# Storing the last four field pairs of every second tile through DMAs of 123, 3 and 2 rows

## The chip, the cores and the metric

The kernel runs on one core of a Trainium2 chip. The metric is the device time of one launch in microseconds (us), the median of three runs. Profiled executions are single ones, and their own time is given beside them.

The core has five engines with their own instruction streams: PE (TensorE, matrix products), DVE (VectorE), ACT (ScalarE), POOL (GpSimd) and SP (SyncE, which here only issues DMAs). Data moves between HBM and the on-chip memory SBUF through 16 DMA engines. To keep them apart from the compute engines, the text calls them **lanes**. A DMA of 128 rows is cut into 8 rows for each of the 16 lanes, each lane works through its share in order, and the DMA has landed when the last of its lanes is done.

## The reference

```python
# x: (2048, 32, 64) f32, W: (496, 64, 64) f32, one matrix for each pair i < j of the 32 fields
xi = x[:, pi, :]
xj = x[:, pj, :]
proj = jnp.einsum('bpd,pod->bpo', xi, W)
return proj * xj
```

For each of the 496 pairs (i, j) the kernel projects field i with the pair's matrix and multiplies the result, element by element, with field j. The output has 2048 x 496 x 64 numbers in f32, 260 MB, against 25 MB of input.

## The kernel before

The batch is cut into 16 tiles of 128 rows. The matrices (`w_sb`) are loaded once and stay in SBUF. For each tile the 32 fields (`x_sb`, two buffers) are turned on PE with an identity (line 268), copied to `x_t` by ACT (line 234), and then go through 21 steps. A step fills two units of PSUM (`proj`, 128x1024 each): one for an even field, one for an odd one (line 290).

The products are made in two ways. DVE multiplies a unit straight from PSUM into the staging buffer (line 332). For about two thirds of the steps (`pool_steps`) the second unit is copied by ACT into the staging buffer (line 256) and multiplied there by POOL (line 219).

The steps form 11 groups with 61, 57, 53, 49, 45, 41, 37, 33, 54, 38 and 28 pairs. A group's pairs lie side by side in the output, so one DMA stores them: 128 rows, of 15,616 bytes each for group 0 and 7,168 bytes each for group 10. SP issues these stores in the order of the groups (line 189), one tile after the other, and waits before each for the engines that make the group (lines 184 to 188). The next tile's fields are loaded by a DMA that ACT issues (line 243).

There are nine staging buffers, called slots, for the eleven groups: groups 9 and 10 use the slots of groups 4 and 5 again (`SHARED_SLOTS`, line 17). Before a group is written into a slot, DVE and ACT wait until the slot's earlier stores have landed (`slot_free`, line 162). Each landed DMA adds 16 to the slot's semaphore `stored[k]`:

```python
eng.wait_ge(stored[k], tile.number * 16 * slot_uses[k] + 16 * len(before))
```

So in each tile group 9 waits for the landing of group 4's store of the same tile, and group 5 of the next tile waits for group 10's store. At the end SP waits for all the stores (line 207).

Of the kernel before, what the change touches and what calls it, by code (L numbers as in the profile page):

```python
# [9 lines left out]
P = 128  # L10
# [4 lines left out]
WARM_UP = 16  # L15

SHARED_SLOTS = {9: 4, 10: 5}


def pair_index(i, j, fields):  # L20
# [51 lines left out]
def field_pair_project(nc, x, w, ident, out, fields, dim):  # L72
    batch = x.shape[0]
    tiles = batch // P
# [11 lines left out]
    def items(tile):  # L86


        for n, item in enumerate(last_tile if tile.last else whole_tile):
            yield item, (1 + n) % 2, tile.number * per_tile + (1 + n) // 2  # L90
# [5 lines left out]
    def group_range(g):  # L96
        segments = [seg for s in groups[g] for unit in steps[s] for seg in unit]
        first = min(pair_index(i, j, fields) for i, j, _ in segments)
        assert sum(n for _, _, n in segments) == max(
            pair_index(i, j, fields) + n for i, j, n in segments) - first  # L100
        return first, sum(n for _, _, n in segments)

    slot_of = [SHARED_SLOTS.get(g, g) for g in range(len(groups))]
    slots = len(groups) - len(SHARED_SLOTS)
    assert sorted(set(slot_of)) == list(range(slots))
    slot_uses = [slot_of.count(k) for k in range(slots)]
# [12 lines left out]
    def every_tile(emit):  # L119

        for t in range(tiles):
            emit(Tile(t, t % 2, t // 2, last=t == tiles - 1))
# [9 lines left out]
    with ExitStack() as ctx:  # L132
        def sb(name, shape, dt=F32):
            return ctx.enter_context(nc.sbuf_tensor(name, shape, dt))

        def sem(name):
            return ctx.enter_context(nc.semaphore(name))
# [7 lines left out]
        staged = [sb(f"staged{k}", [P, slot_pairs[k] * dim]) for k in range(slots)]  # L145
# [12 lines left out]
        stored = [sem(f"stored{k}") for k in range(slots)]  # L158
# [3 lines left out]
        def slot_free(eng, tile, g):  # L162

            k = slot_of[g]
            before = [h for h in range(g) if slot_of[h] == k]
            if not (tile.first and not before):
                eng.wait_ge(stored[k], tile.number * 16 * slot_uses[k] + 16 * len(before))

        def staged_part(s, i, j, n):
            g = group_of[s]  # L170
# [3 lines left out]
        @block.sync  # L174
        def _(sp):
            def emit(tile):
                where = {item: (b, use) for item, b, use in items(tile)}
                for g, group in enumerate(groups):
                    first, n = group_range(g)


                    pooled = any(s in pool_steps for s in group)
                    if pooled and g == 0:
                        sp.wait_ge(pool_scaled[g], tile.number + 1)
                    b, use = where[group[-1]]
                    sp.wait_ge(emptied[b][group[-1] not in pool_steps], use + 1)
                    if pooled and g > 0:
                        sp.wait_ge(pool_scaled[g], tile.number + 1)  # L188
                    sp.dma_start(out[bass.ds(tile.number * P, P), first * dim:(first + n) * dim],
                                 staged[slot_of[g]][:, 0:n * dim]).then_inc(stored[slot_of[g]], 16)  # L190

            half = fields * dim // 2
            sp.dma_start(x_sb[0][:, 0:half], x[0:P, 0:half]).then_inc(x_first_loaded[0], 16)
            sp.dma_start(w_sb[:, w_cuts[0]:w_cuts[1]], w[:, w_cuts[0]:w_cuts[1]]).then_inc(w_loaded[0], 16)
            sp.dma_start(x_sb[0][:, half:], x[0:P, half:]).then_inc(x_first_loaded[1], 16)
            for c in range(1, len(w_cuts) - 2):
                sp.dma_start(w_sb[:, w_cuts[c]:w_cuts[c + 1]], w[:, w_cuts[c]:w_cuts[c + 1]]
                             ).then_inc(w_loaded[c], 16)

            c = len(w_cuts) - 2  # L200
            sp.dma_start(w_sb[0:dim, w_cuts[c]:w_cuts[c + 1]], w[0:dim, w_cuts[c]:w_cuts[c + 1]]
                         ).then_inc(w_loaded[c], 16)
            sp.dma_start(x_sb[1][:], x[P:2 * P, :]).then_inc(x_loaded[1], 16)

            every_tile(emit)
            for k in range(slots):
                sp.wait_ge(stored[k], 16 * slot_uses[k] * tiles)

        @block.gpsimd
        def _(pool):  # L210
# [17 lines left out]
        def _(act):  # L228
# [8 lines left out]
            def load_x(tile):  # L237

                _, b, use = list(items(Tile(tile.number - 1, 1 - tile.parity, None)))[-1]

                act.wait_ge(emptied[b][1], use + 1)
                act.wait_ge(pool_scaled[group_of[pool_steps[-1]]], tile.number)
                act.dma_start(x_sb[1 - tile.parity][:], x[bass.ds((tile.number + 1) * P, P), :]
                              ).then_inc(x_loaded[1 - tile.parity], 16)

            def emit(tile):
                for item, b, use in items(tile):
                    if item == LOAD_BEFORE and not tile.first and not tile.last:
                        load_x(tile)
                    if item == "turn":  # L250
                        turned_out(b, use, 1 - tile.parity)
                    elif item in pool_steps:
                        (i, j, n), = steps[item][1]
                        slot_free(act, tile, group_of[item])
                        act.wait_ge(filled[b][1], use + 1)  # L255
                        nc.scalar.activation(staged_part(item, i, j, n), proj[b][1][:, 0:n * dim],  # L256
                                             ACT.Copy).then_inc(emptied[b][1], 1)
# [58 lines left out]
        @block.vector  # L316
        def _(dve):
            def emit(tile):
                if tile.first:
                    for h in range(2):  # L320
                        dve.wait_ge(x_first_loaded[h], 16)
                for item, b, use in items(tile):
                    if item == "turn":
                        continue
                    slot_free(dve, tile, group_of[item])
                    for h in range(2):
                        if h and item in pool_steps:
                            continue
                        dve.wait_ge(filled[b][h], use + 1)  # L329
                        segments = steps[item][h]  # L330
                        for (i, j, n), at in zip(segments, place(segments, dim)):
                            last = nc.vector.tensor_tensor(  # L332
                                staged_part(item, i, j, n), proj[b][h][:, at:at + n * dim],
                                x_sb[tile.parity][:, j * dim:(j + n) * dim], ALU.mult)
                        last.then_inc(emptied[b][h], 1)

            every_tile(emit)
# [30 lines left out]
```

## Time and profile before

| | us |
|---|---|
| three runs | 690.97 to 691.70, median 691.17 |
| profiled execution | 690.77 |
| its span, first to last instruction | 689.0 |
| busy in it: PE / DVE / POOL / ACT | 597.5 / 414.4 / 390.8 / 205.2 |
| DMA packets' time, queue of SP and queue of ACT, as a share of 16 lanes' span | 93.5% and 5.7% |
| moved | 285.24 MB, mean 414 GB/s |

A busy figure of a compute engine says how long it was at work, not that the kernel had to wait for it. The share of the DMA lanes is a mean over the 16, so 6% of a stretch can mean one lane at work and fifteen idle. One row of one DMA is one packet in this kernel; the record of a packet overlaps the next one's on the same lane a little, so that the share of a fully busy stretch reads as 101% or 102%.

### The profile page before, as it was taken

To read this page: it belongs to the slowest core of one execution; us is meant where nothing else is said; L and a number is where in the kernel's file an instruction comes from. 1 tells how busy PE (TensorE), PEld (TensorE's weight loads), DVE (VectorE), ACT (ScalarE), POOL (GpSimd) and SP (SyncE) were. 2 spreads that over 40 slices of the span, in tenths; PEclk is the share of its full clock that TensorE was granted. 3 is DMA by queue.
4 is the path that set the end of the run, shared out by engine and by line. 5 is a ranking of instruction groups with operands and counts; after the bars stand their busy time and mean duration, and the time that the engine had idled before them with its cause. 6 is when DMAs were issued, how large, how long until landed. Compare 5 with 4: busy or idle time off the path is not lost.

```text
span 689.0 us, 7597 instructions
## 1 busy us (share of the span) xinstructions
PE 597.5 (87%) x2704; PEld 371.1 (54%) x2704; DVE 414.4 (60%) x528; ACT 205.2 (30%) x257; POOL 390.8 (57%) x228
## 2 busy tenths in 40 slices
PE   6969979799797989979799797989979799797972
PEld 4545655465464646646466564645646466464541
DVE  1647657485574756646576574856647576474851
ACT  2312414133241332414233241322414224141320
POOL 0745747566473755738557474755738557374751
PEclk9998989899897998989899898997989989898995
DMA  8999999999999999999999999999999999999897
GB/s 337 382 432 425 432 427 425 427 428 426 420 417 428 424 422 417 427 424 417 427 414 426 408 428 424 412 423 389 420 421 412 428 413 425 411 426 426 363 419 308
DMA packets 29765, 285.24 MB, mean 414 GB/s; under 512 B 3312, under 2 KB 3440, under 8 KB 7216
## 3 DMA queue, kind: packets, MB, share of 16 engines
q1 hardware_dynamic: 27584, 270.28, 93.5%
q10 hardware_dynamic: 2160, 14.75, 5.7%
q14 instruction: 16, 0.13, 0.0%
q8 instruction: 5, 0.08, 0.0%
HBM read 24.97 MB, written 260.05 MB: 414 GB/s over the span
## 4 chain that ended last, share of the span: by engine, by line
PE 48%; DMA 37%; POOL 5%; ACT 4%; DVE 3%; issue 1%; ACTq 0%; DVEq 0%; SPq 0%
PE proj L290 48%; DMA out_dram<-staged 36%; POOL staged L219 5%; ACT staged L256 4%; DVE staged L332 3%; DMA ident_sb<-ident_dram 1%; PE proj L307 1%; PE proj L268 0%; ACT x_t L234 0%; ACTq L255 0%; DVEq L132 0%; SPq L188 0%; DVEq L329 0%
## 5 line engine op out<-in xcount | busy, mean ns | idle before, releaser
L290 PE MATMUL proj<-w_sb,x_t 64*128 64x512 f32 (+7 forms) x2432 | 564.2, 564 | 71.8 <-DVE staged L332 69.5
L332 DVE TENSOR_TENSOR staged<-proj,x_sb 128x1024 f32<-128x1024 f32 (+7 forms) x528 | 414.4, 827 | 263.6 <-PE proj L290 186.4
L219 POOL TENSOR_TENSOR staged<-staged,x_sb 128x1024 f32<-128x1024 f32 (+4 forms) x224 | 390.6, 1755 | 283.1 <-ACT staged L256 281.4
L290 PEld LDWEIGHTS proj<-w_sb,x_t 64*128 64x128 f32 x2432 | 339.6, 205 | 289.3 <-issue 123.6
L256 ACT ACTIVATE staged<-proj 128x1024 f32<-128x1024 f32 (+4 forms) x224 | 172.9, 787 | 455.1 <-PE proj L290 348.1
L234 ACT ACTIVATE x_t<-proj 128x1024 f32<-128x1024 f32 x32 | 31.0, 1020 | 10.3 <-PE proj L268 9.8
L268 PEld LDWEIGHTS proj<-ident_sb,x_sb 128*128 128x128 f32 x256 | 28.2, 142 | 9.7 <-issue 7.6
L268 PE MATMUL proj<-ident_sb,x_sb 128*128 128x128 f32 x256 | 31.8, 278 | 1.5 <-DMA x_sb<-x_dram 1.5
L307 PE MATMUL proj<-ident_sb 128*128 128x128 f32 x16 | 3.7, 424 | 5.6 <-DMA ident_sb<-ident_dram 5.6
L307 PEld LDWEIGHTS proj<-ident_sb 128*128 128x128 f32 x16 | 3.3, 227 | 5.6 <-DMA ident_sb<-ident_dram 5.6
L234 ACT ACT_TABLE_LOAD x1 | 1.3, 1283 | 1.2 <-PEq L362 1.2
L362 POOL MEMSET const-float32-0.0<- 128x1 f32 x1 | 0.1, 98 | 0.2 <-issue 0.2
L362 POOL MEMSET const-bfloat16-1.0<- 128x1 bf16 x1 | 0.1, 101 | 0.0
L362 POOL MEMSET const-uint8-127<- 128x1 uint8 x1 | 0.1, 101 | 0.0
L362 POOL MEMSET const-float32-1.0<- 128x1 f32 x1 | 0.1, 98 | 0.0
## 6 DMA issues: line engine op xcount, KB each, us to landing
out_dram<-staged SPq DMA_DIRECT2D x16, 1952.0 KB, 11.4
out_dram<-staged SPq DMA_DIRECT2D x16, 1824.0 KB, 13.9
out_dram<-staged SPq DMA_DIRECT2D x16, 1728.0 KB, 17.0
out_dram<-staged SPq DMA_DIRECT2D x16, 1696.0 KB, 14.7
out_dram<-staged SPq DMA_DIRECT2D x16, 1568.0 KB, 14.1
out_dram<-staged SPq DMA_DIRECT2D x16, 1440.0 KB, 15.4
out_dram<-staged SPq DMA_DIRECT2D x16, 1312.0 KB, 15.5
out_dram<-staged SPq DMA_DIRECT2D x16, 1216.0 KB, 13.8
```

What stands on the lines that cost most here:

```text
L219: last = nc.gpsimd.tensor_tensor(product, product, x_sb[tile.parity][:, j * dim:(j + n) * dim], ALU.mult)
L234: nc.scalar.activation(x_t[to][:, h * (UNIT // P):(h + 1) * (UNIT // P), :].rearrange("p k b -> p (k b)"), proj[b][h][:], ACT.Copy).then_i ...
L256: nc.scalar.activation(staged_part(item, i, j, n), proj[b][1][:, 0:n * dim], ACT.Copy).then_inc(emptied[b][1], 1)
L268: last = nc.tensor.transpose(proj[b][h][:, n * P:(n + 1) * P], x_sb[of][:, k * P:(k + 1) * P], ident_sb[:])
L290: last = nc.tensor.matmul(proj[b][h][:, at:at + width], x_t[tile.parity][half, i // 2, :], w_sb[half, col:col + width], start=True, stop=True)
L307: nc.tensor.transpose(proj[1][0][:, 0:P], ident_sb[:], ident_sb[:])
L332: last = nc.vector.tensor_tensor(staged_part(item, i, j, n), proj[b][h][:, at:at + n * dim], x_sb[tile.parity][:, j * dim:(j + n) * dim], ...
L362: nc = bacc.Bacc("TRN2", target_bir_lowering=False, num_devices=1)
```

## The change

In tiles 1, 3, ..., 15 (`tile.parity`) group 10 is stored in four DMAs in the place of one. The first takes 24 of its 28 pairs for all 128 rows, now 6,144 bytes a row. The last four pairs, 1,024 bytes a row, follow in DMAs of 123, 3 and 2 rows. A DMA of 123 rows runs on 3 lanes with 41 rows each, one of 3 rows on 3 lanes, and one of 2 rows on 2 lanes, so the four pairs of an odd tile stay off the other lanes. Even tiles are stored as before. The semaphore counts are raised for the three DMAs more.

```diff
+SPLIT_GROUP = 10
+SPLIT_PAIRS = 4
+SPLIT_ROWS = (123, 3, 2)
...
         def slot_free(eng, tile, g):
...
-                eng.wait_ge(stored[k], tile.number * 16 * slot_uses[k] + 16 * len(before))
+
+                more = tile.half * len(SPLIT_ROWS) * (slot_of[SPLIT_GROUP] == k)
+                eng.wait_ge(stored[k], 16 * (tile.number * slot_uses[k] + more + len(before)))
...
-                    sp.dma_start(out[bass.ds(tile.number * P, P), first * dim:(first + n) * dim],
-                                 staged[slot_of[g]][:, 0:n * dim]).then_inc(stored[slot_of[g]], 16)
+                    whole = n - SPLIT_PAIRS if g == SPLIT_GROUP and tile.parity else n
+                    sp.dma_start(out[bass.ds(tile.number * P, P), first * dim:(first + whole) * dim],
+                                 staged[slot_of[g]][:, 0:whole * dim]).then_inc(stored[slot_of[g]], 16)
+                    if whole < n:
+                        row = 0
+                        for rows in SPLIT_ROWS:
+                            sp.dma_start(
+                                out[bass.ds(tile.number * P + row, rows), (first + whole) * dim:(first + n) * dim],
+                                staged[slot_of[g]][row:row + rows, whole * dim:n * dim]
+                            ).then_inc(stored[slot_of[g]], 16)
+                            row += rows
...
             for k in range(slots):
-                sp.wait_ge(stored[k], 16 * slot_uses[k] * tiles)
+                more = tiles // 2 * len(SPLIT_ROWS) * (slot_of[SPLIT_GROUP] == k)
+                sp.wait_ge(stored[k], 16 * (slot_uses[k] * tiles + more))
```

The change moves instructions on SP alone. At the seam from the last tile but one into the last, SP's stores stood like this (`staged5` is the slot of groups 5 and 10, `128x1792` are 128 rows of 1,792 numbers):

```order
L189 DMA out_dram<-staged4 128x2432
L189 DMA out_dram<-staged5 128x1792
```

Those are groups 9 and 10 of any tile. In the changed program the last tile ends so:

```order
L197 DMA out_dram<-staged4 128x2432
L197 DMA out_dram<-staged5 128x1536
L202 DMA out_dram<-staged5 123x256
L202 DMA out_dram<-staged5 3x256
L202 DMA out_dram<-staged5 2x256
```

Nothing changed places. One store became narrower, and three short ones stand behind it. In the odd tiles before the last, group 0's store of the next tile (`staged0`) comes after them.

## Rows read from the trace of the kernel before

**Rows 1.** The page: span, DMA by slices of the span, packets.

```profile
span 689.0 us, 7597 instructions
...
DMA  8999999999999999999999999999999999999897
GB/s 337 382 432 425 432 427 425 427 428 426 420 417 428 424 422 417 427 424 417 427 414 426 408 428 424 412 423 389 420 421 412 428 413 425 411 426 426 363 419 308
```

**Rows 2.** The page: the chain of work that ended last, by engine.

```profile
PE 48%; DMA 37%; POOL 5%; ACT 4%; DVE 3%; issue 1%; ACTq 0%; DVEq 0%; SPq 0%
```

**Rows 3.** That chain in order of time, one tile (start us, us, what).

```profile
533.19 15.18 DMA out_dram<-staged
548.38 0.02 issue
548.40 0.90 DVE staged L332
549.30 0.04 issue
549.35 14.98 PE proj L290 x50
...
564.41 1.03 ACT staged L256
...
565.48 5.79 PE proj L290 x22
...
572.37 2.10 POOL staged L219
...
574.52 15.21 DMA out_dram<-staged
```

**Rows 4.** Windows of one tile each: length, engines' busy time, PEclk, DMA share, GB/s.

```profile
75.70:117.00 41.30, 37.76 (x175) 23.46 (x173) 25.93 (x33) 13.64 (x18) 25.34 (x15) 0.92 1.01 428
...
282.60:324.00 41.40, 37.51 (x172) 23.14 (x170) 25.93 (x33) 12.99 (x17) 24.64 (x15) 0.92 1.00 421
...
530.70:572.00 41.30, 37.38 (x170) 23.14 (x169) 25.93 (x33) 12.72 (x17) 24.35 (x15) 0.92 1.00 420
572.00:613.40 41.40, 37.45 (x172) 23.27 (x171) 25.93 (x33) 12.99 (x17) 24.69 (x15) 0.92 1.01 421
```

**Rows 5.** The same view: a seam between tiles, and the last stores.

```profile
560.50:561.00 0.50, 0.50 (x6) 0.38 (x3) 0.50 (x1) 0.00 (x0) 0.50 (x1) 1.00 0.63 163
680.00:682.00 2.00, 0.00 (x0) 0.00 (x0) 0.00 (x0) 0.00 (x0) 0.00 (x0) 0.50 1.02 431
684.80:687.80 3.00, 0.00 (x0) 0.00 (x0) 0.00 (x0) 0.00 (x0) 0.00 (x0) 0.50 0.06 26
```

**Rows 6.** DMA view, the first 5 us: ACT's queue, rows of 512 bytes.

```profile
q10 hardware_dynamic: 143, 0.07, 5.1%
```

**Rows 7.** DMA view, 8 to 20 us: loads of the matrices.

```profile
DMA packets 1098, 5.04 MB, mean 420 GB/s; under 512 B 121, under 2 KB 121, under 8 KB 1098
...
q1 hardware_dynamic: 1098, 5.04, 102.1%
```

**Rows 8.** DMA view, 680 to 683 us: the last stores.

```profile
DMA packets 162, 1.28 MB, mean 428 GB/s; under 512 B 16, under 2 KB 16, under 8 KB 77
...
q1 hardware_dynamic: 162, 1.28, 102.2%
```

**Rows 9.** Waits from 530 to 571.3 us, one tile: total, times, longest.

```profile
DVE staged L332 <- DMA out_dram<-staged: 4.1, 1, 4.1
PE proj L290 <- DVE staged L332: 3.8, 1, 3.8
```

**Rows 10.** The issuing queue SP: its waits in the whole run.

```profile
SPq L188 <- POOL staged L219: 425.1, 144, 9.8
```

**Rows 11.** Line 189, the stores: what an issue takes (ns, min/median/max).

```profile
L189 SPq DMA_DIRECT2D out_dram<-staged x176: 332/332/384, 20.1 to 678.1; - x176
```

## The prediction
> **What bounds the kernel now.** I begin with the page's slices. The DMA lanes are at 9 tenths or more in nearly all of them, and the kernel moves 410 to 430 GB/s in most of them [rows 1]. The chain that ended last names PE for 48% and DMA for 37% [rows 2], which would make PE the larger part, so the chain has to be read in order of time. In one tile it runs: group 4's store, issued at 533.19, lands 15.18 us later; DVE can then reuse its slot, and 14.98 + 5.79 us of PE work follow until the next tile's group 4 is ready at 574.5 [rows 3]. But a store's own bytes don't take 15 us: group 4 is 128 x 11,520 bytes = 1.47 MB, 3.4 us at 431 GB/s. The other 12 us are its queue. The compute engines run ahead of the stores by that much and then stand until a slot comes free: DVE 4.1 us and PE behind it 3.8 us in a tile [rows 9]. So the loop turns at the pace of the stores, 41.3 to 41.4 us a tile [rows 4], and PE's 37.4 to 37.8 us beside it have room.
>
> The next question is what sets the stores' pace: all 16 lanes, or one of them. The end of the kernel tells it. From 680 to 682 us the lanes move 431 GB/s at a share of 1.02, that is 26.9 GB/s for each lane. From 684.8 to 687.8 us the share is 0.06 and the rate 26 GB/s [rows 5]: one sixteenth. For the last 3.0 us **one lane works alone**, with 3.0 x 26 = 78 KB still to store, while fifteen have nothing left. Every lane was given the same bytes, so this one is slower or was held up.
>
> The tiles say how much slower. Tile 1 moved 428 GB/s, the later ones 420 or 421 [rows 4]. 421 GB/s is 16 x 26.3, the rate of the lone lane as far as its two digits go. I read it so: at first the fast lanes run ahead of the slow one, and once the slots hold them back, everybody moves at the slow lane's pace. The seam at 560.5 us, with a share of 0.63 for half a microsecond [rows 5], is a place where fast lanes run dry while the slow one still has a backlog. A landing counts when the last lane is done, so all the slot waits are waits for that lane.
>
> **What the fast lanes have to spare.** A tile is 421 GB/s x 41.35 us = 17.4 MB, 1.09 MB a lane. At 26.9 GB/s a fast lane needs 40.4 us for it, and has 0.95 us to spare; in a pair of tiles (the change acts once a pair) it needs 80.8 of 82.7 us and spares 1.9.
>
> **The change, part by part.**
>
> *Off every lane.* In an odd tile each lane's 8 rows of group 10 shrink by 1,024 bytes, 8,192 bytes in all. On the slow lane that is 8.19 / 26.3 = 0.31 us, on a fast one 0.30 us. With 8 odd tiles the slow lane's work falls by 8 x 0.31 = **2.5 us**. If it sets the pace before and after, that is the gain.
>
> *Onto three lanes.* They get 41 rows of 1,024 bytes; then 1 row each, then 1 row on two of them: 43, 43 and 42 packets. No packet of 1,024 bytes is in the trace, so I bound it. From below, its bytes alone at 26.9 GB/s take 38 ns. For the likely value I use a line through three sizes: 512-byte rows, 5.1% of 16 lanes x 5 us = 4.1 us over 143 packets, 28.5 ns [rows 6]; 4.6 KB, 102.1% of 192 us over 1098, 178.5 ns [rows 7]; 7.9 KB, 102.2% of 48 us over 162, 303 ns [rows 8]. The slopes are 0.037 and 0.038 ns a byte, so 1,024 bytes record 47 to 48 ns. The records overlap (the 2.1% over full are 4 ns a packet in rows 7), which leaves **43 ns**. From above I take 60 ns, twice the smallest packet seen, since a store's short rows go to HBM and those of rows 6 came from it. Then 43 packets are 1.85 us, and the three lanes' net burden is 1.85 - 0.30 = 1.55 us a pair of tiles (1.3 at 38 ns, 2.3 at 60).
>
> *Does it fit?* The three lanes now need 80.8 + 1.55 = 82.35 us a pair, the slow lane 82.7 - 0.31 = 82.39. They just fit. In the last tile there is no load of x, and there the fast lanes are 3 us ahead at the end, so the final 1.85 us on three lanes end before the slow lane does. The sum stands at -2.5 us, with little margin: break-even with the kernel before is at (82.7 - 80.5) / 43 = 51 ns a packet.
>
> *On SP.* 24 issues more, of 0.33 us each [rows 11]: 8 us on a queue that waits 425 us for POOL alone [rows 10]. The next tile's group 0 store is queued behind them by 1.0 us in every second seam. The slow lane has a backlog then and doesn't notice; a fast lane that has run dry does, and loses what it had to spare. I price it at nothing; were it all on the path, it would be 7 x 1.0 = 7 us.
>
> *The waits.* Group 5 of the next tile now waits for the three short DMAs too. They are on lanes that were ahead by microseconds, and group 10's own share on the slow lane lands after them. PE's and DVE's work is unchanged, and PE's 3.8 us a tile cover a gain of 0.15 us a tile.
>
> **Sum.** Against the profiled execution: 690.8 - 2.5 = 688.3 us. Its time is 0.4 us under the median of the three runs, so I forecast **688.7 us** for the median, 0.36% less.
>
> **The rivals.**
>
> *The slow lane is one of the three.* Then its work grows by 1.85 - 0.31 = 1.54 us in each odd tile, nothing hides it, and the kernel takes 8 x 1.54 = 12.3 us more: 703.5 us. This is the mechanism that makes the change slower. It decides from the first odd tile on. No row here has the number of a lane. Blind, the chance is 3 in 16; times 0.8 that the slow lane is one fixed lane all through, 0.15. The Trainium skill's page "DMA: Bandwidth & Descriptors" bears on it: in "Why a DMA increments its semaphore by 16 and not by 1" it takes the number of lanes as the largest divisor of the rows up to 16 and puts them on the lowest-numbered ones, and in "Latency and other measured facts" it says engines 7 and 15 are usually slower than the others, with a guess at a cause that would not apply to DMAs issued by SP. By the two together the three lanes would be 0 to 2 and this rival would all but fall. The trace shows a slow lane, but not which.
>
> *The three lanes are overfull.* At 60 ns a packet they need 80.8 + 2.3 = 83.1 us a pair, 0.4 more than the slow lane did before: 8 x 0.4 = 3 us slower, 694.2. Between 47 and 55 ns, or with a part of SP's 7 us on the path, gain and loss cancel to within 1.4 us of the time before, and that is 0.2%, about what a measurement of this kernel tells from no change. For it speaks how little margin the sum has, against it the straight line through rows 6 to 8. The skill speaks against the change here: the same page, "Rules for kernel authors", wants a row count that is a multiple of 16 so that all engines work, and calls transfers under 64 KB mostly overhead. In the trace the nearest thing is the small DMA of rows 6, whose packets fit the line, so I don't follow it. I give 0.04 to slower by over 0.2%, and 0.10 to no difference.
>
> *The lane isn't the bound.* The late lane might be only the last to have been served, with the pace set by the loop of group 4, PE and POOL. Then 8 KB fewer on it are worth nothing, 691.2 us. Against it stand the 12 us of queue in a 15 us landing. The same time comes out if the DMA of 123 rows is spread over all lanes. 0.03 for both.
>
> **How the numbers follow.** Forecast 0.68, no difference 0.13, overfull lanes 0.04, slow lane among the three 0.15. So faster 0.68, same 0.13, slower 0.19. The forecast's own range is 687.9 (the 2.5 us and 0.3 us of scatter, and up to 0.5 us that shorter slot waits might add) to 689.8. Taking in no difference and the beginning of overfull lanes it reaches to 692.5; what is left out is the slow lane among the three and most of the overfull case, under 0.2 together.
>
> **What would show it.** Right: the tiles' period falls from 41.35 to about 41.2 us in the mean, the late tiles move about 422 GB/s, and the lone lane's stretch at the end is about as long as before or shorter, with a step before it where three lanes work on (share 0.25 or so). The seams of odd tiles have fewer dry lanes. Wrong by the slow lane: tile pairs of 84 us, group 4's landing some 1.5 us later after each odd tile, and a tail of some microseconds with a share near 0.19 or 0.06 behind the fast lanes' end. Wrong by overfull lanes: a tail with a share near 0.19, from three lanes, longer than 2 us. Wrong by price: packets of 1 KB at well over 48 ns recorded.

## The result, and the profile after

The changed kernel takes 693.77 us, the median of 7 runs from 690.43 to 695.91; the kernel before took 690.83 beside it (7 runs, 690.68 to 691.70). The ratio is 1.0041, with a 95% interval of 1.0025 to 1.0056: **slower by 0.4%**, where 0.36% faster was forecast. Two things stand out. The sign is wrong, and the runs spread over 5.5 us where those of before stay within 1.0.

The profiled execution is the fastest of the seven, 690.43 us. It is still 2.1 us above the sum of the prediction. The page of the changed kernel answers to [rows 1] so:

```profile
span 688.6 us, 7621 instructions
...
DMA  8999999999999999999999999999999999999996
GB/s 341 400 429 424 432 427 426 428 408 428 422 429 427 406 428 423 428 426 416 428 411 425 405 420 422 404 424 411 428 426 411 426 409 427 418 420 420 383 419 285
DMA packets 30853, 285.24 MB, mean 414 GB/s; under 512 B 3376, under 2 KB 4528, under 8 KB 8304
...
q1 hardware_dynamic: 28672, 270.28, 93.6%
```

The bytes and the mean rate are those of before. The last digit is new: the last slice, 17 us long, is at 6 tenths and 285 GB/s, where before it stood at 7 and 308. The chain's shares are the old ones [rows 2]:

```profile
PE 48%; DMA 37%; POOL 5%; ACT 4%; DVE 3%; issue 1%; ACTq 0%; DVEq 0%; SPq 0%
```

In order of time, the chain through one tile of the changed kernel (start us, us, what) has the same pieces as [rows 3] too. A store is 15.4 or 15.7 us from issue to landing, with PE's work between two of them:

```profile
531.49 15.36 DMA out_dram<-staged
...
547.81 14.51 PE proj L307 x50
...
563.49 5.79 PE proj L307 x22
...
572.52 15.71 DMA out_dram<-staged
```

So the loop is what it was. Windows of the changed kernel, for the same four tiles as [rows 4] and then for the last stores (length, engines' busy time, PEclk, DMA share, GB/s):

```profile
75.70:117.00 41.30, 38.37 (x174) 23.44 (x173) 25.94 (x33) 13.66 (x18) 25.34 (x15) 0.92 1.01 426
282.60:324.00 41.40, 36.90 (x171) 22.79 (x172) 26.03 (x34) 12.95 (x18) 24.67 (x15) 0.92 1.01 422
530.70:572.00 41.30, 37.21 (x172) 23.11 (x169) 25.94 (x33) 13.03 (x17) 24.67 (x15) 0.92 1.01 418
572.00:613.40 41.40, 36.96 (x171) 23.12 (x169) 25.94 (x33) 12.99 (x17) 24.66 (x15) 0.92 1.01 421
680.00:682.00 2.00, 0.00 (x0) 0.00 (x0) 0.00 (x0) 0.00 (x0) 0.00 (x0) 0.50 0.99 411
682.00:684.00 2.00, 0.00 (x0) 0.00 (x0) 0.00 (x0) 0.00 (x0) 0.00 (x0) 0.50 0.31 121
684.00:685.00 1.00, 0.00 (x0) 0.00 (x0) 0.00 (x0) 0.00 (x0) 0.00 (x0) 0.50 0.26 66
685.00:686.00 1.00, 0.00 (x0) 0.00 (x0) 0.00 (x0) 0.00 (x0) 0.00 (x0) 0.50 0.21 77
686.00:687.00 1.00, 0.00 (x0) 0.00 (x0) 0.00 (x0) 0.00 (x0) 0.00 (x0) 0.50 0.12 42
687.00:688.60 1.60, 0.00 (x0) 0.00 (x0) 0.00 (x0) 0.00 (x0) 0.00 (x0) 0.50 0.02 5
```

The tiles move 418 to 426 GB/s, no more than before, though the slow lane has 0.31 us less to do in every second tile. The end tells why. Before, one lane worked alone for 3.0 us at a share of 0.06 [rows 5]. Now four lanes are busy from 684 to 685 us (0.26), three to four in the next microsecond (0.21), and two in the one after (0.12). Three lanes have caught up with the slow one: the last short row ends 1.5 us behind the last wide one. In the stretch from 684 to 685 four lanes move 66 GB/s, 16 GB/s each. Short rows alone don't explain so little (1,024 bytes in 42 ns are 24 GB/s). Two rows of 6,144 bytes, each with short rows behind it on its lane, take 0.89 and 1.19 us there in the place of 0.23.

What DVE and PE wait for in a tile (530 to 571.3 us) stayed, against [rows 9]:

```profile
DVE staged L349 <- DMA out_dram<-staged: 4.3, 1, 4.3
PE proj L307 <- DVE staged L349: 4.0, 1, 4.0
```

And SP's waits in the whole run, with its short stores (ns, min/median/max), against [rows 10, 11]:

```profile
SPq L195 <- POOL staged L236: 425.9, 144, 8.3
...
L202 SPq DMA_DIRECT2D out_dram<-staged x24: 579/810/1239, 99.0 to 679.2; - x24
```

A short store holds SP for 810 ns, not for 332.

### The profile page after: what moved, and what is told of

The parts are those of the page before. It is cut to its first block, busy times and chain, and to the rows that moved or that the text cites. A ratio compares the mean times of both kernels' runs of the same rounds, so it can differ in the third digit from the quotient of the medians.

```text
span 688.6 us, 7621 instructions
## 1 busy us (share of the span) xinstructions
PE 597.1 (87%) x2704; PEld 370.5 (54%) x2704; DVE 414.5 (60%) x528; ACT 205.4 (30%) x257; POOL 390.8 (57%) x228
## 4 chain that ended last, share of the span: by engine, by line
PE 48%; DMA 37%; POOL 5%; ACT 4%; DVE 3%; issue 1%; ACTq 0%; DVEq 0%; SPq 0%
PE proj L307 48%; DMA out_dram<-staged 37%; POOL staged L236 5%; ACT staged L273 4%; DVE staged L349 3%; DMA ident_sb<-ident_dram 1%; PE proj L324 1%; PE proj L285 0%; ACT x_t L251 0%; ACTq L272 0%; DVEq L137 0%; SPq L195 0%; DVEq L346 0%
## 6 DMA issues: line engine op xcount, KB each, us to landing
out_dram<-staged SPq DMA_DIRECT2D x16, 1824.0 KB, 14.2
```

## The experiments

Every kernel was timed beside the kernel before on the same chip. The experiments ran on five chips: the same kernel again, seven, fifteen and all lanes, three pairs, and both four-lane forms on one; five lanes, two and eight pairs, and the short DMAs behind group 0 on a second; the kernels without loads and with full rows on three more. The median of the kernel before lay between 690.59 and 690.81 us on all of them. Differences below are of medians. The 1,024-byte rows record 46 ns in the changed kernel, so 42 ns net of the overlap. What a lane gets more in a pair of tiles, less what the narrower store takes off it, is called its **net burden**: 43 x 0.042 - 0.31 = 1.50 us for the change.

### The same kernel again

> The changed kernel once more, to see a slower run's trace than the one on record (690.4 us; the seven runs lie between 690.4 and 695.9). Theory A (the three lanes are overfull in most runs): median 692 to 695 us, and at the end of the trace a stretch of 2 us or more with a DMA share near 0.19, falling to 0.06, in which the short rows of 1,024 bytes are stored. Rival B (the slow lane still ends last, and SP's longer issues delay it): the tail is one lane at share 0.06 storing rows of 6,144 bytes, and the short rows end before it.

No edit. 692.59 us, ratio 1.0028 [1.0015, 1.0040]: slower again, by 2.0 us. Its trace shows the mechanism more plainly than the first. Windows of the last stores:

```profile
680.00:682.00 2.00, 0.00 (x0) 0.00 (x0) 0.00 (x0) 0.00 (x0) 0.00 (x0) 0.50 0.92 387
...
686.00:687.00 1.00, 0.00 (x0) 0.00 (x0) 0.00 (x0) 0.00 (x0) 0.00 (x0) 0.50 0.29 89
687.00:688.00 1.00, 0.00 (x0) 0.00 (x0) 0.00 (x0) 0.00 (x0) 0.00 (x0) 0.50 0.24 58
688.00:689.00 1.00, 0.00 (x0) 0.00 (x0) 0.00 (x0) 0.00 (x0) 0.00 (x0) 0.50 0.13 45
```

Four lanes work on at 687 us with 58 GB/s, 15 GB/s each against the 26.9 GB/s that a lane moves in wide rows. Here too two rows of 6,144 bytes take 0.73 and 1.02 us. From tile 7 on, the last short row of an odd tile ends 1.24 to 1.84 us behind the last wide one. 1.84 is 43 rows of 43 ns, so there the burdened lane was the last one in the wide store already: its lead was gone.

### Which lane is the slow one

The rows of the short stores steer them: 119 rows go to 7 lanes, 125 to 5, 120 to 15, 64 and 32 to all 16.

```diff
-SPLIT_ROWS = (123, 3, 2)
+SPLIT_ROWS = (119, 7, 2)      # seven lanes; (125, 3) five, (120, 8) fifteen, (64, 32, 32) all
```

> The short DMAs have 119, 7 and 2 rows: 7 lanes with 17 rows each, then 1 and 1. Burden per burdened lane and pair of tiles: 19 packets x 0.042 = 0.80 less 0.30 = +0.5 us in the place of +1.5; the other nine lanes are relieved as in the change. Theory A: no burdened lane is overfull any more and the relieved slow lane gives the whole 2.5 us, 688.0 to 689.5 us, if the slow lane is not among the seven; if it is, 8 x 0.5 = 4 us slower, 695. Rival B (SP's issues): 692 to 695 us.

694.67 us, 4.1 more than before (ratio 1.0060 [1.0046, 1.0074]). A lane that gets 18 short rows has a net burden of 18 x 0.042 - 0.31 = 0.45 us, and 8 x 0.45 = 3.6: on a fast lane that would be hidden, so the slow lane is one of the seven.

> The short DMAs have 125 and 3 rows: five lanes with 25 rows each, three of them one more, so 26 x 0.043 - 0.30 = +0.8 us for a burdened lane and pair of tiles. The run with seven lanes put the slow lane among lanes 0 to 6, and the change with three left it out. If it is one of the five (lane 3 or 4): 8 x 0.8 = 6.5 us over the kernel before, 697 us, and in each odd tile the last short row ends 1.1 us after the last wide one. If it is lane 5 or 6: it is relieved, no burdened lane is overfull, 688.5 to 690.5 us.

696.63 us, 5.8 more (1.0092 [1.0077, 1.0107]). Lanes 3 and 4 get 25 rows here and 0 to 2 get 26, so 25 x 0.042 - 0.31 = 0.74 us, times 8 is 5.9. The slow lane is among the five, and it carries that whole burden. The trace agrees: in the seams of odd tiles the last short row ends 1.06 us behind the last wide one, which is 25 rows of 42 ns. Not being among the three of the change (else those runs would stand at 8 x 1.5 = 12 us), it is 3 or 4 on this chip.

> Two short DMAs, 120 rows on 15 lanes with 8 rows each, 8 rows on 8 lanes. Only one lane is relieved of the 8 KB in an odd tile, the highest one; eight lanes carry 1 KB more, seven carry the same as before. If the slow lane is that highest one: 688 to 689.5 us. If it is another: 690.5 to 692 us. Rival B (SP's issues, two in the place of three): 692 to 694 us.

692.44 us, 1.8 more (1.0022 [1.0013, 1.0031]).

> The three short DMAs have 64, 32 and 32 rows, so each runs on all 16 lanes, and the number of DMAs and SP's issues stay as in the change. No lane is relieved and none is burdened. Theory A (lanes): the kernel before's time within 1 us, 690 to 692, and as little scatter as before (1 us). Rival B (SP's issues of 0.8 us each in the seam cost the time): 692 to 695 us, as the change.

692.07 us, 1.5 more (1.0021 [1.0012, 1.0030]). In these two the slow lane is not spared (with fifteen, only the last lane is), and 8 or 9 short rows in the place of 8 x 1,024 bytes should cost 0.2 to 0.6 us in all. There is about 1.2 us more, which the short DMAs cost as such, wherever they run. At the end one lane is alone again, as in the kernel before (windows of the all-lanes form):

```profile
686.00:687.00 1.00, 0.00 (x0) 0.00 (x0) 0.00 (x0) 0.00 (x0) 0.00 (x0) 0.50 0.09 34
687.00:689.00 2.00, 0.00 (x0) 0.00 (x0) 0.00 (x0) 0.00 (x0) 0.00 (x0) 0.50 0.06 25
```

### How much fits on the fast lanes

Fewer pairs leave fewer bytes for the three lanes, and 124 + 4 rows put them on four.

```diff
-SPLIT_PAIRS = 4
+SPLIT_PAIRS = 2      # also 3 and 8; SPLIT_ROWS = (124, 4) for four lanes
```

> The change with two pairs (512 bytes a row) in the place of four. The three lanes get 43 x 0.024 - 0.15 = +0.9 us a pair of tiles, the others are relieved by 0.15. Theory A (three overfull lanes cost the time): they aren't overfull any more, and the time is 689.5 to 691 us with the kernel before's small scatter, and the last lane at the end stores wide rows. Rival B (SP's issues or the number of DMAs): as the change, 692 to 694 us.

689.80 us, 1.0 less than before (0.9988 [0.9979, 0.9997]).

> The change with three pairs (768 bytes a row) on three lanes: burden 43 x 0.033 - 0.23 = +1.2 us a pair of tiles. Theory A: the spare time of the fast lanes read off the other runs (change +0.3 us a pair over it at a burden of 1.5) is 1.2 us a pair, so this one stands at the edge: 690 to 691.5 us, between two pairs (689.8) and four (692.6 to 693.8). If the spare time were the 1.9 us of the prediction, 8 x 0.23 = 1.8 us off: 689.0 us.

689.67 us, 1.0 less (0.9987 [0.9978, 0.9996]; 12 executions, one of which took 1,044 us). That is a miss: at 1.2 us of spare time 690 to 691.5 was expected, at 1.9 us 689.0, and the result lies between.

> The four pairs of the change through DMAs of 124 and 4 rows: four lanes with 32 packets each, burden 32 x 0.042 - 0.30 = +1.05 us a pair of tiles in the place of 1.5. If the slow lane is lane 4: the relief of 0.31 a pair is whole, the four lanes stay within 1.2, and the time is 688.5 to 690 us, so the change's loss was its three lanes' burden. If it is lane 3: 8 x 1.05 = 8.4 us over the kernel before, 699 us.

689.90 us, 0.8 less (0.9996 [0.9984, 1.0007]): no difference, with the four pairs of the change and the same relief, only spread over four lanes. It also names the slow lane. Were it lane 3, this form would cost 8 x (32 x 0.042 - 0.31) = 8.3 us; so on this chip, where the seven lanes held it, it is lane 4, 5 or 6. With the 3 or 4 of the chip of the five lanes that is **lane 4**, if it is the same lane on both chips, which no run shows.

> Three pairs (768 bytes a row) through DMAs of 124 and 4 rows: four lanes with 32 packets each. The run with five lanes put the slow lane at lane 3 or 4. Burden 32 x 0.033 - 0.23 = +0.8 us a pair of tiles, relief 0.23. If the slow lane is lane 4: it is relieved, and the four lanes are less burdened than the three in the two-pair run (0.9), so 8 x 0.23 = 1.8 us off less what two more DMAs cost: 689.0 to 690.0 us, faster than the kernel before and than two pairs on three lanes. If it is lane 3: 8 x 0.8 = 6.7 us over the kernel before, 697 us.

689.29 us, 1.4 less (0.9978 [0.9969, 0.9987]): the lowest median of all, ahead of both kernels; its interval overlaps those of two and three pairs on three lanes. Windows of its last stores:

```profile
682.00:684.00 2.00, 0.00 (x0) 0.00 (x0) 0.00 (x0) 0.00 (x0) 0.00 (x0) 0.50 0.71 232
684.00:685.00 1.00, 0.00 (x0) 0.00 (x0) 0.00 (x0) 0.00 (x0) 0.00 (x0) 0.50 0.24 88
685.00:686.00 1.00, 0.00 (x0) 0.00 (x0) 0.00 (x0) 0.00 (x0) 0.00 (x0) 0.50 0.08 31
686.00:687.00 1.00, 0.00 (x0) 0.00 (x0) 0.00 (x0) 0.00 (x0) 0.00 (x0) 0.50 0.05 19
```

Here the last short row ends at 685.3 us, and one lane is left (0.08, 0.05), as forecast for the change.

> The change with eight pairs (2,048 bytes a row). The three lanes get 43 x 0.080 - 0.61 = +2.8 us a pair of tiles. Theory A: they are overfull from the second odd tile on; against the change 8 x (2.8 - 1.5) = 10 us more, 702 to 704 us, and short rows are stored alone on three lanes at the end of the odd tiles. Rival B (SP's issues): 692 to 694 us, since their number is the same.

706.55 us, 15.7 more (1.0231 [1.0211, 1.0251]), and more than the 702 to 704 us expected. Its tiles alternate (windows from one tile's end to the next; after an even tile, an odd one, an even one):

```profile
396.70:436.80 40.10, 37.09 (x175) 22.91 (x172) 25.94 (x35) 12.75 (x16) 24.40 (x14) 0.95 0.96 400
436.80:482.20 45.40, 36.69 (x168) 22.49 (x167) 25.83 (x34) 12.75 (x16) 24.44 (x14) 0.86 1.00 411
482.20:522.30 40.10, 37.08 (x174) 22.93 (x172) 25.97 (x34) 12.75 (x16) 24.40 (x14) 0.95 0.97 400
```

45.4 + 40.1 = 85.5 us a pair against 82.7. PE's time is the same in both, so this is the lanes' doing.

The six forms side by side; the last column is the spare time that would explain the measurement, net burden less an eighth of the difference. A lane's number of rows and the relief are worked out from the row counts and from 26.3 GB/s:

| pairs, lanes | row, ns recorded | relief a pair, us | net burden a pair, us | against before, us | spare, us |
|---|---|---|---|---|---|
| 3, four | 36 | 0.23 | 32 x 0.032 - 0.23 = 0.79 | -1.4 | at least 0.97 |
| 2, three | 27 | 0.16 | 43 x 0.023 - 0.16 = 0.83 | -1.0 | at least 0.95 |
| 4, four | 46 | 0.31 | 32 x 0.042 - 0.31 = 1.03 | -0.8 | 1.13 |
| 3, three | 36 | 0.23 | 43 x 0.032 - 0.23 = 1.15 | -1.0 | 1.28 |
| 4, three (the change) | 46 | 0.31 | 1.50 | +2.0, +2.9 | 1.25, 1.13 |
| 8, three | 84 | 0.62 | 43 x 0.080 - 0.62 = 2.82 | +15.7 | 0.85 |

The lightest two burdens give most of their relief (8 x 0.23 = 1.8 and 8 x 0.16 = 1.3 us), and from 1.0 us of net burden on, ever less of it comes. All rows agree on a spare time between 0.9 and 1.3 us a pair. The prediction had 1.9. The column leaves out what short DMAs cost as such; with the 1.2 us of the all-lanes form, 0.15 us a pair, it would read 1.0 to 1.4.

### The order on SP

The three short DMAs are issued behind group 0 of the next tile.

```diff
-    if whole < n: (the short stores, behind group 10)
+    if whole < n: short[:] = [tile, first, whole, n, slot_of[g]]
+    if short and (tile.last if g == SPLIT_GROUP else g == 0): issue_short()
```

> The change with the three short DMAs issued behind the next tile's group 0 store in the place of ahead of it; the lanes' loads are the same. Theory A: no difference from the change but for what SP's 2.4 us cost in the seam, 691.5 to 693.5 us. Rival B (the three issues delay the group 0 store, whose lanes run dry): the time falls to the kernel before's or below, 688.5 to 691 us.

694.75 us, 3.9 more than before (1.0056 [1.0038, 1.0073]); neither theory had so much. If the short issues had held group 0 up, this would have mended it. It didn't. In the traces of before and of the change alike, group 0 is issued 5.5 to 7.1 us behind group 10, and the short issues are over by 3.9 us.

### Full rows in the place of short ones

In odd tiles group 10 is stored as 112 rows of 7,168 bytes for all lanes, and the other 16 rows in small DMAs of full rows.

```diff
-SPLIT_ROWS = (123, 3, 2)
+SPLIT_ROWS = (3, 3, 3, 3, 3, 1)      # three lanes; (4, 4, 4, 4) four lanes
...
+rows = P - sum(SPLIT_ROWS) if g == SPLIT_GROUP and tile.parity else P
+(store rows 0 to rows - 1, then for each of SPLIT_ROWS that many rows more)
```

> Here the rows that go to three lanes are not short: in an odd tile group 10 is stored as 112 rows of its full 7,168 bytes for all lanes and five DMAs of 3 rows and one of 1 row behind it. Every lane but three is relieved of one row, 0.27 us; one of the three gets five rows more than before, two of them four, 1.1 to 1.3 us a pair of tiles. The change gave its three lanes 1.55 us. Theory A, the three lanes have only about 1.2 us a pair to spare, whatever kind of work it is: between 0 and +1 us of the kernel before. Theory B, the spare time is the 1.9 us of the prediction and what fails is the short rows (1,024 bytes, dearer when others store too): 8 x 0.27 = 2.1 us faster than before.

> As the run with three lanes and full rows, but the last 16 rows go out in four DMAs of 4 rows: four lanes get three rows more than before, 0.8 us a pair, all others one row less. Both theories let 0.8 us fit and expect the full relief, 8 x 0.27 = 2.1 us faster than before. If it comes out at no gain, the cost is in the number of DMAs or in the waits for one more set of lanes, not in the lanes' work.

704.91 us (1.0216 [1.0189, 1.0243]) and 703.07 us (1.0162 [1.0137, 1.0187]): 14.2 and 12.4 us more, which neither theory had. The issues on SP in the two, three lanes and then four:

```profile
L200 SPq DMA_DIRECT2D out_dram<-staged x48: 241/1020/1967, 100.4 to 692.4; - x48
```

```profile
L200 SPq DMA_DIRECT2D out_dram<-staged x32: 745/1262/3015, 98.2 to 693.2; - x32
```

Four issues of 1.26 us, or six of 1.02, are 5 to 6 us, as much as the gap that SP has behind group 10: in most odd seams group 0 is issued 0.1 us behind the last of them. In the second kernel's odd seams from tile 7 on the first row of group 0 starts 9.1 to 9.6 us behind the issue of group 10, in its even ones 6.6 to 7.8. These two therefore don't tell short rows from long ones: the number of DMAs got in between. They do show what the prediction's 7 us on SP look like when they come true: some 2 us in each of the last four odd seams, an estimate of 9 of the 15.7 us by which this profiled execution is longer.

### Without the loads of x

Five kernels leave out the loads of x for all tiles but the first two, so that the products of later tiles are computed from old fields. The waits for these loads go with them; nothing else is left out.

```diff
-                act.wait_ge(emptied[b][1], use + 1)
-                act.wait_ge(pool_scaled[group_of[pool_steps[-1]]], tile.number)
-                act.dma_start(x_sb[1 - tile.parity][:], x[bass.ds((tile.number + 1) * P, P), :]
-                              ).then_inc(x_loaded[1 - tile.parity], 16)
+                return
...
-                        pe.wait_ge(x_loaded[1 - tile.parity], 16 * tile.half + 16)
+                        if tile.first:
+                            pe.wait_ge(x_loaded[1], 16)
```

> The kernel before without the 14 loads of x that ACT issues (lines 241 to 244): tiles 2 to 15 compute with the x of tiles 0 and 1, and the output is that of those. Every lane is rid of 8 x 0.305 = 2.44 us a tile: 690.7 - 14 x 2.44 = 656.5 us if the slow lane sets the pace, and its fingerprint (0.15 us over the others in a wide store) stays. It is the base for the next run.

> The changed kernel without those 14 loads, the same data left out. Theory C (a lane that comes early to the load of x pays for it: its first packets take 0.5 to 2 us in the place of 0.31, so the fast lanes have only 1.2 us a pair of tiles to spare and not 1.9): without the loads the spare time is the slow lane's own 1.0 us a tile, 2.0 a pair, the three lanes' 1.5 fit, and this kernel is faster than the one without loads and without the change by 1.5 to 2.5 us, 654 to 655 us, with little scatter. Rival D (the spare time is small for a reason in the stores themselves, or the short DMAs cost it): slower than that one by 2 to 3 us, as with the loads, 658.5 to 659.5 us.

657.26 us without the change and 664.55 with it: 7.3 us apart, more than the 2.0 to 2.9 with the loads. Neither theory had so much. It speaks against the thought that the lanes lose their spare time to the load of x, but a cost comes in here that the kernels with loads hardly have, as the next lines show. Windows of the changed kernel without loads, two tiles and then the first 2 us of group 0 behind the odd tile 9:

```profile
408.70:449.80 41.10, 34.63 (x161) 21.32 (x159) 23.77 (x29) 12.14 (x16) 24.45 (x14) 0.88 1.00 410
449.80:487.60 37.80, 36.85 (x179) 22.61 (x179) 27.92 (x39) 13.36 (x17) 24.41 (x14) 0.99 0.99 416
...
417.55:419.55 2.00, 2.00 (x12) 0.99 (x8) 1.78 (x3) 0.34 (x1) 1.96 (x1) 1.00 0.98 312
```

And of the kernel before without loads, the same places:

```profile
408.70:447.70 39.00, 37.64 (x180) 22.67 (x177) 27.82 (x39) 13.56 (x17) 24.40 (x14) 0.98 0.96 402
447.70:486.70 39.00, 34.74 (x161) 21.48 (x159) 23.87 (x30) 11.94 (x16) 24.42 (x14) 0.90 1.01 423
...
417.70:419.70 2.00, 2.00 (x13) 1.31 (x12) 1.70 (x2) 0.93 (x1) 0.94 (x1) 1.00 1.18 494
```

A pair of tiles takes 78.9 us against 78.0. In the seam the lanes of the changed kernel are as busy as ever, at 0.98, but at 312 GB/s: 20 GB/s a busy lane, against 26 in the other (494 over 16 x 1.18). Some thirteen lanes have a first row of group 0 that takes up to 1.2 us longer than its 0.58. A full share is no proof that lanes move what they can.

> Leaves out the loads of x of all tiles but the first two, and stores the four pairs of odd tiles in DMAs of 64, 32 and 32 rows on all 16 lanes. No lane is burdened more than another. Against the kernel before without those loads (657.3 us): if the 7.3 us that the change cost without the loads came from short DMAs as such, this is near 664; if they came from the three lanes' burden, it is 657 to 659 (the all-lanes form cost 1.5 us with the loads).

The edit is the rows (64, 32, 32). 658.30 us, 1.0 more than without the change (measured on another chip; the kernel before differed by 0.1 us between the two). So of the 7.3 us the short DMAs as such are 1.0 (their own sum has 0.2), and 6.3 come from putting them on three lanes.

> Leaves out the loads of x of all tiles but the first two, and issues the three short DMAs of an odd tile behind the next tile's group 0, whose rows then enter every lane's queue first. Without the loads the change takes 664.6 us against 657.3 for the kernel before, and the other lanes' first packets of group 0 are stretched in the seams after odd tiles. Theory H, group 0 is held up because its rows are issued behind the short rows of lanes that are late: the stretched packets go and the time falls to 657 to 660 us. Theory S, the three lanes simply carry more than they have to spare, wherever their rows stand in the queue: about 664.6 us as before.

665.31 us, as with the short DMAs ahead of group 0 (664.55, runs from 663.41 to 665.83). In this trace the long first rows of group 0 are gone, and the time is not. So it isn't the place ahead of group 0 that costs (theory H). But the long rows have only moved along with the short ones: now some 40 rows of group 1 in a seam are lengthened, by up to 1.2 us. A window of 2 us in it, the same tile:

```profile
423.60:425.60 2.00, 2.00 (x15) 1.21 (x12) 1.49 (x2) 0.80 (x1) 2.00 (x2) 1.00 1.04 305
```

To see what that is worth, add up over the stores of a pair of tiles (from tile 3 on) what each row takes beyond the median of its size, and divide by 16 lanes. Without loads it is 0.2 us a lane in the kernel before, 1.3 in the change and 1.3 with the short DMAs behind group 0, and 0.4 with the short DMAs on all lanes. The change costs 7.3 / 8 = 0.9 us a pair, the all-lanes form 0.1. So without the loads most of the loss can be these lengthened rows, on nearly all lanes, and not the work of three. Theory S, that the three lanes simply carry more than they have to spare, isn't needed for it and isn't shown by it.

> Leaves out the loads of x of all tiles but the first two, and stores three pairs of odd tiles in DMAs of 124 and 4 rows on four lanes (32 rows of 768 bytes a lane; net burden about 0.9 us a pair of tiles, against 1.55 in the change). With the loads this form was 1.5 us faster than the kernel before. Theory S with about 1.2 us to spare: it fits, and the relief of 0.23 us in each of 8 odd tiles shows: 657.3 - 1.8 = 655.5 us. If it is slower than 657.3 us, the lanes have less to spare without the loads, or any short rows in the seam hold group 0 up (theory H).

657.31 us, the time of the kernel before without loads (657.26) and 1.8 us above what theory S gave with 1.2 us to spare. Nothing of the relief shows. Read by theory S alone, the lanes would have less to spare without the loads: 1.50 - 7.3/8 = 0.6 us by the one kernel, some 0.8 by the other. The lengthened rows (0.65 us a lane and pair here, 0.2 in the kernel before) are the rival, and can make up the missing 0.23 us a pair.

## Why the prediction was wrong

*What bounds the kernel* was right. One lane sets the pace: burdening it with 0.45 and 0.74 us a pair costs 4.1 and 5.8 us, about eight times as much, and relieving it with two or three pairs gains.

*What the fast lanes have to spare* is **the step that failed**. It took a lane's rate from the undisturbed last stores (26.9 GB/s, [rows 5]), divided a tile's bytes by it, and got 0.95 us of spare time a tile, 1.9 a pair. Six burdens on three or four lanes give 0.9 to 1.3 us a pair. The change asks for 1.5. That lies between the two figures, so a term that was 0.7 us too large turned a gain of 2.5 into a loss of 2 to 3: where the lanes are overfull, each pair costs 1.50 - 1.2 = 0.3 us more than before, 8 x 0.3 = 2.4 us. The comparison of 82.35 with 82.39 us rested on this difference of two nearly equal numbers, read from rows of two and three digits. An error of 1% in the rate is 0.8 us of 80.8.

*Off every lane* was right in size, as the forms that fit show: three pairs on four lanes gained 1.4 of 1.8 us.

*Onto three lanes* was right. 1,024-byte rows record 46 ns where the line through three sizes gave 47 to 48.

*On SP* was wrong in its numbers, though not the cause. A short issue takes 810 ns and not 332, and the row that would have said so stood in the trace of before: a load issued right behind another held SP for 580 ns.

```profile
L203 SPq DMA_DIRECT2D x_sb<-x_dram x1: 580/580/580, 8.7 to 8.7; - x1
```

The issues of [rows 11] never follow one another at once. The three short ones end at most 3.9 us behind group 10's issue and group 0 comes at 5.5 to 7.1 us, so nothing is late, and putting them behind group 0 didn't help. Short DMAs as such do cost about 1 us in 16 tiles, by the all-lanes forms with loads and without; that was priced at nothing.

*The rivals.* "The slow lane is one of the three" did not happen: by the five, seven and four lanes it is none of lanes 0 to 2, and lane 4 if both chips have the same. The prediction set beside its blind chance of 0.15 the Trainium skill, "DMA: Bandwidth & Descriptors", section "Why a DMA increments its semaphore by 16 and not by 1", for the lowest-numbered lanes; the row counts behave by that rule (+4.1 us with 119 rows, +5.8 with 125, -0.8 and -1.4 with 124), though no trace here has a lane's number. The same page's section "Latency and other measured facts" calls engines 7 and 15 usually the slower ones; here, by the row counts, it was neither. "Three lanes overfull" is what happened, at 0.04 the least of the rivals. Its price of 60 ns a row was not met, its break-even at 51 ns neither; with 1.2 us to spare the break-even is at (1.2 + 0.31) / 43 = 35 ns, below any value that the prediction's bounds held. The chances were drawn over the price of a row alone, while the spare time had no bounds of its own. The range ended at 692.5 and left the result out by 1.3 us.

*What would show it* named the sign that came: a tail in which three lanes work on beside or behind the slow one.

**What stays open** is why the lanes have 1.2 us and not 1.9. Shown are two things that it is not: the place of the issues on SP (two kernels) and the packets' own length (46 ns). The loads of x are not cleared, since without them the lengthened rows came in. With the loads these rows are few: in the first trace of the change 12 to 25 of group 0's 128 rows are lengthened by 0.06 to 0.4 us after each of the odd tiles 7 to 13 (in the second trace 5, 16, 18 and none), after even tiles none. Added up as above they are 0.6 us a lane and pair in the change and 0.6 in the four-lane form of the same four pairs, against 0.4 in the kernel before (and 1.0 and 1.1 in the two kernels with full rows). The two forms lie 2.8 us or more apart, so what separates them is the work on the burdened lanes and not these rows; the 0.2 us above the kernel before may be part of what short DMAs cost as such. What lengthens the rows was not settled. Nor was a kernel tried that gives three lanes more work without any more DMAs.

## What to carry to other kernels

Spare time that comes out as a small difference of two long times is the number to bound first: give it its own low and high value, and if the change needs more than the low one, forecast by that. A row count steers a DMA onto few lanes, so first find the slow lane with one run each of 4, 5 and 7 lanes on one chip, and then load the others to half of what the trace seems to leave them. Each small DMA also costs its issue, which right behind another one is two to four times as long.

## What the runs showed of the hardware

One lane is slower than the others: it works alone for 3.0 us at the end of the kernel before, and by the estimate from its 26.3 GB/s against 26.9 it is about 1 us late in 41. By the row counts it is not among the first three on either of two chips, and number 4 if it is the same on both. DMA issues on SP took 332 ns where the queue had been idle, and short ones back to back 0.6 to 1.6 us, with all sixteen lanes as well as with three (with full rows up to 3.0 us); the all-lanes form:

```profile
L202 SPq DMA_DIRECT2D out_dram<-staged x24: 972/1246/1572, 100.0 to 682.3; - x24
```

In seams in which three lanes store short rows, rows of 14,592 and 15,616 bytes on nearly all lanes took up to 1.2 us longer than their usual 0.55 and 0.58 us, whether the short DMAs stood ahead of group 0 or behind it. The two kernels without loads show this, at a full DMA share.

The forms that lose time scatter more in single runs: 5.5 us in the change and 4.7 in the form with eight pairs, against 1.0 in the kernel before beside the change and 1.2 in the four-lane form with three pairs. Why was not shown.
